# A recurrent mixer in finer steps, its groups four steps apart, with affines and norm scalings on ScalarE and its bias products among the expert tiles of the stage before

## The chip, the cores and the metric

One core of a Trainium2 chip. The time is the device time of one execution in microseconds, the median over several executions of the same program. Stretches of the program are given in microseconds from the first instruction of the profiled execution.

## The reference, cut to what matters

The whole is a decoder of two layers on x of 16 x 128 x 256 (2048 tokens of 256 features), everything in float32. The parts that the change touches are the end of the first layer and the recurrent mixer that opens the second:

```python
out = jnp.einsum('bse,bsem->bsm', gate, y)          # 2 of 16 experts; y holds the bias b2 of each
x = _layernorm(x + out)

xn = _ln(x, ln1_g, ln1_b)
xp = _shift(xn)                                     # the token before
k = (xn * mix_k + xp * (1.0 - mix_k)) @ Wk          # likewise v, and r under a sigmoid
wkv = _wkv(k, v, time_decay, time_first)            # a = ew*a + exp(k)*v; b = ew*b + exp(k); a / (b + 1e-8)
x = x + r * wkv @ Wo
yn = _ln(x, ln2_g, ln2_b)
yp = _shift(yn)
kk = jnp.square(jax.nn.relu((0.5 * yn + 0.5 * yp) @ Wfk))
rr = jax.nn.sigmoid(yn @ Wfr)
x = _layernorm(x + (x + rr * (kk @ Wfv)))           # the outer residual and norm, as the kernel orders them
```

The two layer norms in a row, the one after the experts and the mixer's own ln1, read the same x. The weights that choose an expert's output also weigh its bias: that part is gate (2048 x 16) times b2 (16 x 256), the "bias products" below.

## The kernel before, in words

The kernel writes out every engine's instruction stream by hand, with semaphores between the engines, and divides the program into stages with a barrier on all five queues between them (barrier, L154). An engine carries out its stream in order. Two stages matter.

**The expert stage** (tensor_bank L1021, scalar_bank L1056, vector_bank L1076, gpsimd_bank L1097, sync_bank L1107) works through NT0 = 47 tiles of 128 gathered token rows, each with one expert's weights of 2 MB. Step k of TensorE does the second layer of tile k-5 (bank 6 or 7), the first layer of tile k-3 (banks 2 to 5) and the two transposes of tile k-2 (L1053), which go into bank i % 2 with i = k-2. VectorE, in its step k, applies half of the first layer's relu (four instructions of 128x128, L1086) and then copies the transposes out of their bank (L1095). Results go to the DRAM tensor ys0.

**The mixer** (tensor_mix L1160, scalar_mix L1228, gpsimd_mix L1260, vector_mix L1290) treats the 2048 tokens as four groups of 512 (four blocks of 128 tokens; a group is four sequences). Each group goes through the phases 0 to 13 of steps_e (L1151): step n holds phase n - 2g of group g, so a group runs two steps behind its predecessor. The phases:

- 0, 1: POOL gathers the two expert rows of each token from ys0, eight indirect transfers of 128 rows.
- 2: TensorE multiplies gate by b2 (two banks, two products of 16x128 by 16x256 each); VectorE adds them to X (L1305), adds the eight weighted gathered blocks (L1314), and takes the statistics of the norm (norm_stats L163: four BATCH_NORM_STATS2, four aggregates, variance plus epsilon); POOL raises to the power -0.5 (norm_rstd L176, L181).
- 3: VectorE scales X by the norm (norm_scale L183, L188), takes statistics again; POOL the power. 4: VectorE scales into e_xn.
- 5: TensorE transposes e_xn (na); VectorE applies gain and bias (the affine, L1332), subtracts the token before (L1336) and mixes three times (L1343).
- 6: TensorE multiplies by the k, v and r weights; ScalarE takes exponentials (L1239 to L1244); VectorE multiplies, scans twice (L1354, L1355), adds 1e-8 (L1357), multiplies by 1 + e_r (L1361), takes the reciprocal (L1363) and multiplies (L1368): wkv, in two halves m.
- 7: TensorE's output product (wo); VectorE adds it to X (xi, L1378) and takes statistics, POOL the power. 8: VectorE scales into e_xn; POOL adds xi to X (L1279).
- 9: transposes (nb); VectorE's affine (L1398) and the sum with the token before (hh, L1402).
- 10: TensorE's fk (8 banks) and fr (2 banks); ScalarE relu (L1252) and tanh (L1258); POOL squares (L1288).
- 11: TensorE's fv; VectorE's two steps x4 (L1411, L1414). 12: statistics and power. 13: VectorE scales X (x5).

Banks of PSUM are taken by use (L82), which returns how often the bank was used before; a product then waits until it has been freed as often. In the mixer they go round by eight in TensorE's order. All matmuls are issued through mm (L142), so the profile puts them on L143; one float32 product makes two records.

```python
def steps_e():
    for n in range(20):
        for g in range(4):
            if 0 <= n - 2 * g <= 13:
                yield g, n - 2 * g
```

Of the kernel before, what the change touches and what calls it, by code (L numbers as in the profile page):

```python
# [51 lines left out]
ROWS = ["w2_b", "bo", "br", "gb"]  # L52

# [12 lines left out]
def build(nc, ins, out):  # L66
    with ExitStack() as ctx:
# [1078 lines left out]
        e_th = [alloc(512) for _ in range(2)]  # L1146
        yg_in = [sem(f"yg_in{i}") for i in range(8)]
# [3 lines left out]
        def steps_e():  # L1151
            for n in range(20):
                for g in range(4):
                    if 0 <= n - 2 * g <= 13:
                        yield g, n - 2 * g

        def e_tokens(t, kc, dims):
            return view(t, 516 * kc + dims, [[129, 4], [1, 128]])

        def tensor_mix(t):  # L1160
# [6 lines left out]
            for g, ph in steps_e():  # L1167
                if ph == 2:
                    t.wait_ge(late_in, 64)
                    for b2 in range(2):  # L1170
                        b, n = use(("b2", g, b2), at())
                        t.wait_ge(bank_free[b], n)
                        for i in range(2):
                            c = 4 * g + 2 * b2 + i
                            h = mm(t, banks[b][:, i * 256:(i + 1) * 256], GT[0:16, c * 128:(c + 1) * 128], b2r[0:16, :], True, True)
                        h.then_inc(bank_full[b], 1)
                elif ph in (5, 9):
                    what, ready, src = ("na", xa_done, e_xn[0]) if ph == 5 else ("nb", xb_done, e_xn[1])
                    t.wait_ge(ready, g + 1)
                    for kc in range(2):  # L1180
                        b, n = use((what, g, kc), at())
                        t.wait_ge(bank_free[b], n)
                        for i in range(4):
                            h = t.transpose(banks[b][:, i * 128:(i + 1) * 128], src[:, i * 256 + kc * 128:i * 256 + kc * 128 + 128], ident)
                        h.then_inc(bank_full[b], 1)
                elif ph == 6:
# [8 lines left out]
                elif ph == 7:  # L1195
# [8 lines left out]
                elif ph == 10:  # L1204
# [13 lines left out]
                elif ph == 11:  # L1218
# [9 lines left out]
        def scalar_mix(a):  # L1228
# [3 lines left out]
            for g, ph in steps_e():  # L1232
                if ph == 6:
                    for m in range(2):
# [9 lines left out]
                        a.activation(e_r[m], banks[b], ACT.Exp, scale=-1.0).then_inc(bank_free[b], 1)  # L1244
                elif ph == 10:
# [7 lines left out]
                    for b2 in range(2):  # L1253
# [4 lines left out]
                        a.activation(e_th[b2], banks[b], ACT.Tanh, scale=0.5).then_inc(bank_free[b], 1)  # L1258

        def gpsimd_mix(p):  # L1260
            for i in range(2):
                p.memset(e_XN[i], 0.0).then_inc(xn_pads, 1)
            posi = posi0.bitcast(I32)
            for g, ph in steps_e():
                if ph in (0, 1):
                    for i in range(4):
                        slot = 4 * ph + i
# [4 lines left out]
                elif ph in (2, 3, 7, 12):  # L1272
                    norm_rstd(p, 4)
                elif ph == 8:
# [5 lines left out]
                elif ph == 10:  # L1280
# [9 lines left out]
        def vector_mix(v):  # L1290
            held = {}
# [5 lines left out]
            v.wait_ge(xn_pads, 2)  # L1297
            for g, ph in steps_e():
                xg = xrow(g)
                if ph == 2:  # L1300
                    for b2 in range(2):
                        b, n = U["b2", g, b2]
                        v.wait_ge(bank_full[b], n + 1)
                        xx = X[:, g * 1024 + b2 * 512:g * 1024 + b2 * 512 + 512]
                        v.tensor_tensor(xx, banks[b], xx, ALU.add).then_inc(bank_free[b], 1)  # L1305
                    for kk in range(2):
                        for i in range(4):
                            if kk == 0:
                                b, n = U["b2", g, i // 2]
                                v.wait_ge(bank_free[b], n + 1)  # L1310
                            else:
                                v.wait_ge(summed, 8 * g + i + 1)
# [3 lines left out]
                    held[g] = norm_stats(v, 4, xg)  # L1316
                elif ph == 3:
                    norm_scale(v, held[g], 4, xg, xg).then_inc(vstep.up(), 1)
                    v.wait_ge(vstep.sem, vstep.n)
                    held[g] = norm_stats(v, 4, xg)  # L1320
                elif ph == 4:
# [3 lines left out]
                    norm_scale(v, held[g], 4, xg, lambda i: e_xn[0][:, i * 256:(i + 1) * 256]).then_inc(xa_done, 1)  # L1325
                elif ph == 5:
                    xn = e_XN[0]
                    for kc in range(2):
                        b, n = U["na", g, kc]
                        v.wait_ge(bank_full[b], n + 1)  # L1330
                        v.wait_ge(vstep.sem, vstep.n)
                        v.tensor_scalar(e_tokens(xn, kc, 1), view(banks[b], 0, [[128, 4], [1, 128]]), vcol("g1", kc), vcol("b1", kc), ALU.mult, ALU.add).then_inc(bank_free[b], 1)  # L1332
# [13 lines left out]
                elif ph == 6:  # L1346
                    for m in range(2):
# [8 lines left out]
                        v.wait_ge(vstep.sem, vstep.n)  # L1356
                        v.tensor_scalar(e_b[m], e_b[m], 1e-8, None, ALU.add).then_inc(vstep.up(), 1)  # L1357
# [3 lines left out]
                        v.scalar_tensor_tensor(e_b[m], e_r[m], 1.0, e_b[m], ALU.add, ALU.mult).then_inc(vstep.up(), 1)  # L1361
# [8 lines left out]
                elif ph == 7:  # L1370
                    xi = e_xi[g % 2]
                    if g >= 2:
                        v.wait_ge(xi_added, g - 1)
                        v.wait_ge(xb_done, g - 1)
                    for b2 in range(2):
# [6 lines left out]
                    held[g] = norm_stats(v, 4, lambda i: xi[:, i * 256:(i + 1) * 256])  # L1382
                elif ph == 8:
                    xi = e_xi[g % 2]
                    if g >= 1:
                        b, n = U["nb", g - 1, 1]
                        v.wait_ge(bank_full[b], n + 1)
                    norm_scale(v, held[g], 4, lambda i: xi[:, i * 256:(i + 1) * 256], lambda i: e_xn[1][:, i * 256:(i + 1) * 256]).then_inc(xb_done, 1)
                elif ph == 9:
                    xn = e_XN[1]  # L1390
                    if g >= 1:
                        b, n = U["fr", g - 1, 1]
                        v.wait_ge(bank_full[b], n + 1)
                        v.wait_ge(hh_done, g)
                    for kc in range(2):
                        b, n = U["nb", g, kc]
                        v.wait_ge(bank_full[b], n + 1)
                        v.tensor_scalar(e_tokens(xn, kc, 1), view(banks[b], 0, [[128, 4], [1, 128]]), vcol("g2", kc), vcol("b2", kc), ALU.mult, ALU.add).then_inc(bank_free[b], 1)  # L1398
# [5 lines left out]
                elif ph == 11:  # L1404
# [10 lines left out]
                elif ph == 12:  # L1415
                    v.wait_ge(x4_added, 2 * g + 2)
                    held[g] = norm_stats(v, 4, xg)
                elif ph == 13:
                    norm_scale(v, held[g], 4, xg, xg).then_inc(vstep.up(), 1)
# [666 lines left out]
        NORMS = 48  # L2086
        shift = alloc(16)
        shifted, scaled = sem("shifted"), sem("scaled")
# [59 lines left out]
        def scalar_experts(a):  # L2148
# [24 lines left out]
            for c in range(16):  # L2173
                st = stats[(NORMS + c) % 6]
                a.wait_ge(shifted, c + 1)
# [3 lines left out]
                a.wait_ge(scaled, c + 1)  # L2179
                a.dma_start(out[c * 128:(c + 1) * 128, :], xt2_ring[c % 3]).then_inc(o_out[c % 3], 16)  # L2180

        def vector_experts(v):
# [33 lines left out]
            for u, c in steps_i():  # L2216
                xx = xblock(c)
                if u == "sum":
# [7 lines left out]
                    if c >= 6:  # L2226
                        v.wait_ge(scaled, c - 5)
# [241 lines left out]
```

## Time and profile before

| | us |
|---|---|
| median of three runs | 1712.78 |
| lowest, highest | 1711.32, 1714.36 |
| the profiled execution | 1711.79 |
| its span, first to last instruction | 1709.8 |
| PE (TensorE matmul) busy in it | 1438.0 |
| DVE (VectorE) busy | 916.3 |
| ACT (ScalarE) busy | 542.5 |
| POOL (GpSimd) busy | 514.6 |

The mean granted clock of TensorE was 0.919 of full speed. A chain lists, in order of time, the work that led to the last instruction, each piece with what released the next; "issue" is time in which the engine waited for nothing that the profile shows. In a timeline the bracket gives how long the engine had been idle before an instruction and who ended it. In windows PEclk is the clock that was granted.

### The profile page before, as it was taken

Reading aid. Unit: us, or ns where it says so; the run is one execution under the profiler, and the core shown is the slowest. Engines: PE = TensorE matmul, PEld = TensorE weight load, DVE = VectorE, ACT = ScalarE, POOL = GpSimd, SP = SyncE. Lnnn points to the kernel's source line nnn. Section 1 sums busy time; section 2 is a strip of 40 time slices with the busy share of each in tenths; the row PEclk is TensorE's granted clock in tenths of the full one; section 3 lists DMA queues with packets and bytes.
Section 4 is the critical chain, followed back from the end, with each engine's and each line's share of the span. In section 5 each row is a group of like instructions: output and inputs, shape, how many; then the busy total and the mean of one; then the engine's idle time right before and its main releaser. Section 6 shows DMA issues by size and latency. Waiting matters only on the chain.

```text
span 1709.8 us, 29284 instructions
## 1 busy us (share of the span) xinstructions
PE 1438.0 (84%) x10056; PEld 1108.8 (65%) x10056; DVE 916.3 (54%) x2612; ACT 542.5 (32%) x1377; POOL 514.6 (30%) x506
## 2 busy tenths in 40 slices
PE   7778997569999999646999869988888675999987
PEld 3454676459999999523567535655556443899985
DVE  7353556522222111389776236677768752667655
ACT  4203443212222222000221115443434312666652
POOL 2011000021111110243322211133435473766775
PEclk9888999579999999767999979999999887999998
DMA  7771000079988998110000061112222599655528
GB/s 221 198 239 50 2 15 14 25 291 358 327 319 332 325 326 317 37 50 25 0 1 1 0 177 35 44 65 78 90 80 103 197 317 336 185 175 166 168 69 344
DMA packets 135424, 260.88 MB, mean 153 GB/s; under 512 B 13807, under 2 KB 108043, under 8 KB 129008
## 3 DMA queue, kind: packets, MB, share of 16 engines
q1 hardware_dynamic: 113872, 212.85, 37.0%
q0 software_dynamic: 16800, 39.88, 6.8%
q10 hardware_dynamic: 4608, 6.29, 1.1%
q8 instruction: 82, 1.34, 0.3%
q14 instruction: 62, 0.51, 0.1%
HBM read 197.71 MB, written 52.72 MB: 146 GB/s over the span
## 4 chain that ended last, share of the span: by engine, by line
PE 48%; DVE 10%; issue 8%; POOL 6%; DMA 5%; ACT 1%; SPq 1%; POOLq 0%; ACTq 0%; DVEq 0%
PE bank L143 45%; POOL xe L1556 4%; DMA arena<-in_banka 2%; PE bank L2100 2%; DMA arena<-yr 1%; DVE arena L168 1%; DVE arena L188 1%; DVE arena L1363 1%; POOL arena L1271 1%; DVE arena L1854 1%; SPq L2307 1%; PE bank L1053 1%; POOL arena L181 1%; DVE arena L1844 1%; DMA arena<-xd,arena 0%
## 5 line engine op out<-in xcount | busy, mean ns | idle before, releaser
L143 PE MATMUL bank<-arena 128*128 128x128 f32 (+8 forms) x8728 | 1295.0, 339 | 171.3 <-DMA arena<-in_banka 26.0
L143 PEld LDWEIGHTS bank<-arena 128*128 128x128 f32 (+5 forms) x8728 | 966.7, 181 | 452.2 <-issue 283.4
L181 POOL TENSOR_TENSOR arena<-arena 128x1 f32<-128x1 f32 (+1 forms) x64 | 55.3, 865 | 500.5 <-DVE arena L173 500.5
L1086 DVE TENSOR_SCALAR arena<-bank,arena 128x128 f32<-128x128 f32 x188 | 52.9, 344 | 272.1 <-PE bank L143 272.1
L2241 POOL DMA_INDIRECT yr<-arena x159 | 169.0, 1063 | 95.4 <-ACT arena L2171 49.5
L1105 POOL DMA_INDIRECT arena<-xd,arena x47 | 44.7, 950 | 294.7 <-PE bank L1053 260.9
L1556 POOL DMA_INDIRECT xe<-arena x112 | 113.1, 1010 | 31.6 <-issue 31.5
L2206 DVE COPY arena<-arena 128x768 f32 x127 | 77.0, 607 | 57.2 <-issue 56.9
L1756 ACT ACTIVATE arena<-bank,arena 128x256 f32<-128x256 f32 x128 | 59.0, 472 | 97.7 <-DVE arena L1844 97.7
L1073 ACT ACTIVATE arena<-bank,arena 128x128 f32<-128x128 f32 x188 | 53.7, 368 | 89.8 <-PE bank L143 89.8
L1064 ACT ACTIVATE arena<-bank 128x256 f32<-128x256 f32 x47 | 18.1, 384 | 201.4 <-PE bank L143 201.4
L2171 ACT ACTIVATE arena<-bank,arena 128x256 f32<-128x256 f32 x159 | 73.8, 474 | 23.7 <-PE bank L143 17.7
L2164 ACT ACTIVATE arena<-bank 128x128 f32<-128x128 f32 x143 | 39.7, 278 | 104.9 <-PE bank L143 104.8
L2100 PE MATMUL bank<-arena 128*128 128x128 f32 x318 | 61.1, 282 | 4.3 <-DMA arena<-xe 4.3
L168 DVE BATCH_NORM_STATS2 arena<-arena 128x6 f32<-128x256 f32 x160 | 58.5, 415 | 2.4
L746 DVE TENSOR_REDUCE arena<-bank 128x4 f32<-128x512 f32 x64 | 39.7, 684 | 36.4 <-PE bank L143 36.4
L188 DVE TENSOR_SCALAR arena<-arena 128x256 f32<-128x256 f32 x144 | 53.9, 430 | 10.0 <-POOL arena L181 9.6
L1252 ACT ACTIVATE arena<-bank 128x512 f32<-128x512 f32 x32 | 19.1, 597 | 125.4 <-PE bank L143 97.1
L1796 POOL TENSOR_TENSOR arena<-arena 128x512 f32<-128x512 f32 x16 | 20.3, 1266 | 118.1 <-DVE arena L1835 118.1
L1829 DVE COPY arena<-bank 128x512 f32<-128x512 f32 x16 | 11.1, 692 | 80.2 <-PE bank L143 80.2
L2157 ACT ACTIVATE arena<-bank 128x256 f32<-128x256 f32 x127 | 48.8, 384 | 0.6 <-issue 0.4
L2190 DVE TENSOR_SCALAR arena<-arena 128x1 int32<-128x1 f32 x159 | 32.3, 204 | 27.4 <-DMA arena<-xe 27.3
(243 smaller groups left out, 1371.6 us busy)
## 6 DMA issues: line engine op xcount, KB each, us to landing
arena<-in_bank SPq DMA_DIRECT2D x47, 2052.0 KB
arena<-xe SPq DMA_DIRECT2D x159, 129.0 KB, 2.2
arena<-kd SPq DMA_DIRECT2D x16, 1024.0 KB, 10.9
arena<-arena SPq DMA_DIRECT2D x16, 896.0 KB, 5.4
arena<-in_bank SPq DMA_DIRECT2D x8, 1536.0 KB, 12.0
arena<-yr SPq DMA_DIRECT2D x16, 768.0 KB, 15.0
xe<-arena SPq DMA_DIRECT2D x1, 6321.0 KB, 26.7
ys<-arena SPq DMA_DIRECT2D x47, 128.0 KB, 3.2
```

The lines of the kernel that those rows point to most:

```text
L143: return t.matmul(o, l, r, start=start, stop=stop, skip_group_check=True)
L168: h = v.bn_stats(st[:, 6 * b:6 * b + 6], src(b)).then_inc(vstep.up(), 1)
L181: p.tensor_tensor(st[:, 40:40 + nb], st[:, 32:32 + nb], cc("mhalf", 0, nb), ALU.pow).then_inc(rstd, 1)
L188: h = v.tensor_scalar(dst(b), src(b), st[:, 24 + 2 * b:25 + 2 * b], st[:, 40 + b:41 + b], ALU.subtract, ALU.mult)
L1073: h = a.activation(h_ring[i % 3][:, m * 128:(m + 1) * 128], banks[b][:, m * 128:(m + 1) * 128], ACT.Relu, bias=sbc(w_ring[i % 5], 4096 + m))
L1086: h = v.tensor_scalar(h_ring[i % 3][:, (4 + m) * 128:(5 + m) * 128], banks[b][:, m * 128:(m + 1) * 128], sbc(w_ring[i % 5], 4100 + m), 0.0 ...
L1556: p.indirect_dma_start(xe, bass.IndirectOffsetOnAxis(ap=posi[i][:, at:at + 1], axis=0), stg[i][:, at * RW:(at + 1) * RW], None).then_inc(a ...
L1756: h = a.activation(f_s[g % 2][:, hh * 512 + j * 256:hh * 512 + j * 256 + 256], banks[b][:, j * 256:j * 256 + 256], ACT.Exp, scale=-1.0, bi ...
L2100: h = t.transpose(banks[b][:, (2 * i + j) * 128:(2 * i + j) * 128 + 128], x2_ring[n % NX][:, j * 128:(j + 1) * 128], ident)
L2171: a.activation(y2_ring[n % NY], banks[b][:, 0:256], ACT.Copy, scale=wcol_[:, n:n + 1]).then_inc(bank_free[b], 1)
L2206: v.tensor_copy(e_ring[m % 4], WB[:, bass.ds(at * ROW1, ROW1)]).then_inc(w_copied, 1)
L2241: p.indirect_dma_start(yr, bass.IndirectOffsetOnAxis(ap=sidx.bitcast(I32)[:, n:n + 1], axis=0), y2_ring[n % NY], None, bounds_check=14335, ...
```

## The change

What it does, part by part:

1. **The order.** steps_e goes; a written list MIXER takes its place, of units "0load", "0sum", ... (group, unit). Every engine walks the same list and carries out its part of each unit. A group now stands some four steps behind its predecessor, and a phase is divided into several units.
2. **Biases.** The bias products leave the mixer and are spread over the expert stage, a pair of them at k = 4, 8, ..., 32 behind the transposes, with VectorE's addition behind its copy.
3. **Norms.** The two norms at the start take their statistics once: POOL's power works on eight columns, four for the norm and four for both norms together, with the variance v(1 + eps) + eps^2. Statistics get a buffer for each group and norm.
4. **ScalarE.** The three scalings x3, xb and x5 (four instructions of 128x256) and the two affines (two of 128x512) go to ScalarE, and the 1 + of the sigmoid too. VectorE makes a 128x4 shift for each scaling. The scaling into e_xn ahead of na (xa) stays on VectorE.
5. **wkv.** The 1e-8 is added in the multiplication (one instruction less in each half).
6. **The pads** of e_XN are cleared by VectorE, only where they are read, and no longer by POOL.

```diff
+MIXER = """
+0load 0sum 0xa 0na 0aff 1load 0x3 1sum 0mix 1xa 0kvr 1na 0exp 1aff
+2load 0wkv 1x3 2sum 0wo 1mix 2xa 0xi 1kvr 2na 0xx 1exp 2aff 3load
+0xb 1wkv 2x3 3sum 0nb 1wo 2mix 3xa 0afb 1xi 2kvr 3na 0hh 1xx
+2exp 3aff 0fk 1xb 2wkv 3x3 0sq 1nb 2wo 3mix 0fv 1afb 2xi 3kvr
+0x4 1hh 2xx 3exp 0x5 1fk 2xb 3wkv 1sq 2nb 3wo 1fv 2afb 3xi
+1x4 2hh 3xx 1x5 2fk 3xb 2sq 3nb 2fv 3afb 2x4 3hh 2x5 3fk
+3sq 3fv 3x4 3x5"""
...
(tensor_bank, at the end of step k)
+                for p2 in biases_at(k):
+                    t.wait_ge(late_in, 64)
+                    b, n = use(("b2", p2), k % 2)
+                    t.wait_ge(bank_free[b], n)
+                    for i in range(2):
+                        c = 2 * p2 + i
+                        h = mm(t, banks[b][:, i * 256:(i + 1) * 256], GT[0:16, c * 128:(c + 1) * 128], b2r[0:16, :], True, True)
+                    h.then_inc(bank_full[b], 1)
+        def biases_at(k):
+            return (k // 4 - 1,) if k % 4 == 0 and 0 <= k // 4 - 1 < 8 else ()
...
(vector_bank, at the end of step k)
+                for p2 in biases_at(k):
+                    v.wait_ge(xd0_out, 64)
+                    b, n = U["b2", p2]
+                    v.wait_ge(bank_full[b], n + 1)
+                    xx = X[:, p2 * 512:p2 * 512 + 512]
+                    v.tensor_tensor(xx, banks[b], xx, ALU.add).then_inc(bank_free[b], 1)
...
(scalar_mix)
+            def scaled_by(g, c, src, dst):
+                st = st_of(g, c)
+                a.wait_ge(shifted, shifts[g, c] + 1)
+                for i in range(4):
+                    h = a.activation(dst(i), src(i), ACT.Identity, scale=st[:, 40 + i:41 + i], bias=st[:, 48 + i:49 + i])
+                return h
...
+                        a.activation(e_tokens(e_XN[0], kc, 1), view(banks[b], 0, [[128, 4], [1, 128]]), ACT.Identity, scale=vcol("g1", kc), bias=vcol("b1", kc)).then_inc(bank_free[b], 1)
...
-                        a.activation(e_r[m], banks[b], ACT.Exp, scale=-1.0).then_inc(bank_free[b], 1)
+                        a.activation(e_r[m], banks[b], ACT.Exp, scale=-1.0).then_inc(astep.up(), 1)
+                        a.wait_ge(astep.sem, astep.n)
+                        a.activation(e_r[m], e_r[m], ACT.Identity, bias=cc("ones", 0, 1)).then_inc(bank_free[b], 1)
...
(vector_mix)
-                        v.tensor_scalar(e_b[m], e_b[m], 1e-8, None, ALU.add).then_inc(vstep.up(), 1)
...
-                        v.scalar_tensor_tensor(e_b[m], e_r[m], 1.0, e_b[m], ALU.add, ALU.mult).then_inc(vstep.up(), 1)
+                        v.scalar_tensor_tensor(e_b[m], e_b[m], 1e-8, e_r[m], ALU.add, ALU.mult).then_inc(vstep.up(), 1)
...
+            def shift_of(g, c):
+                st = st_of(g, c)
+                v.scalar_tensor_tensor(st[:, 48:52], view(st, 24, [[2, 4]]), -1.0, st[:, 40:44], ALU.mult, ALU.mult).then_inc(shifted, 1)
```

In the list, "fk" is the fr product too, "sum" holds the gathered sums with their statistics and power, "xi" and "x4" hold theirs, "xx" is POOL's addition of xi to X. TensorE's own order comes out as 0na 0kvr 1na 0wo 1kvr 2na 0nb 1wo 2kvr 3na 0fk 1nb 2wo 0fv 3kvr 1fk 2nb 3wo 1fv 2fk 3nb 2fv 3fk 3fv. The last stage's norm counter starts at 44 instead of 48, and its semaphores shifted and scaled, which the mixer now uses too, at 12 and 4.

## Rows read from the trace of the kernel before

**Rows 1.** Expert stage, ten-microsecond window: busy PE, PEld, DVE, ACT, POOL; clock, DMA, GB/s.

```profile
560.00:570.00 10.00, 10.00 (x70) 9.41 (x69) 2.91 (x10) 2.04 (x7) 1.89 (x2) 1.00 0.94 321
```

**Rows 2.** Chain that ended last, in the expert stage: start us, us, what.

```profile
561.06 0.22 PE bank L1053 x2
561.28 7.03 PE bank L143 x48
```

**Rows 3.** Chain that ended last, in the mixer.

```profile
707.95 1.86 POOL arena L1262 x2
...
818.41 43.21 PE bank L143 x136
...
866.82 41.30 PE bank L143 x136
...
912.48 31.28 PE bank L143 x112
```

**Rows 4.** Timeline, 940 to 990 us: start, us, instruction, idle before.

```profile
943.86 0.69 DVE L1411 SCALAR_TENSOR_TENSOR arena<-arena,bank 128x512 f32<-128x512 f32 x1 [5.46 <-PE bank L143]
...
946.63 1.28 DVE L1402 TENSOR_TENSOR arena<-arena 128x512 f32<-128x512 f32 x2
947.83 1.40 DVE L168 BATCH_NORM_STATS2 arena<-arena 128x6 f32<-128x256 f32 x4
947.96 0.46 PEld L143 LDWEIGHTS bank<-arena 128*128 128x128 f32 x2 [3.58 <-DVE arena L1402]
947.96 32.96 PE L143 MATMUL bank<-arena 128*128 128x512 f32 x112 [3.34 <-DVE arena L1402]
...
949.67 0.17 DVE L173 TENSOR_SCALAR arena<-arena 128x4 f32<-128x4 f32 x1
...
951.91 0.19 PEld L143 LDWEIGHTS bank<-arena 128*128 128x128 f32 x1 [0.24 <-issue]
...
985.63 1.38 DVE L188 TENSOR_SCALAR arena<-arena 128x256 f32<-128x256 f32 x4 [1.12 <-POOL arena L181]
...
988.32 0.23 DVE L1804 CAST arena<-arena 128x128 f16<-128x128 f32 x1 [1.31 <-POOLq L156]
```

**Rows 5.** Half-microsecond windows of L1095, VectorE's copy, alone.

```profile
562.00:562.50 0.50, 0.28 (x1) 1.00 0.92 394
562.50:563.00 0.50, 0.13 (x1) 1.00 1.12 460
```

**Rows 6.** Timeline of all engines from 700 to 760 us.

```profile
729.69 0.95 POOL L1271 DMA_INDIRECT arena<-ys,arena  x1 [0.30 <-issue]
...
735.87 0.95 POOL L1271 DMA_INDIRECT arena<-ys,arena  x1 [0.30 <-DVE arena L1314]
...
741.42 1.53 DVE L1332 TENSOR_SCALAR arena<-bank,arena 128x512 f32<-128x512 f32 x2
...
744.19 4.06 DVE L1343 SCALAR_TENSOR_TENSOR arena<-arena 128x512 f32<-128x512 f32 x6
...
751.65 0.69 DVE L1352 TENSOR_TENSOR arena<-bank,arena 128x512 f32<-128x512 f32 x1
...
754.75 0.45 DVE L1357 TENSOR_SCALAR arena<-arena 128x512 f32<-128x512 f32 x1
```

**Rows 7.** Chain of the stretch from 753 to 835 us.

```profile
760.03 0.69 DVE arena L1352
```

**Rows 8.** Timeline of all engines from 784 to 832 us.

```profile
810.42 3.25 DVE L1314 SCALAR_TENSOR_TENSOR arena<-arena 128x256 f32<-128x256 f32 x8
```

**Rows 9.** Two-microsecond windows: PE busy, PEclk, DMA share, GB/s.

```profile
948.00:950.00 2.00, 2.00 (x3) 0.51 0.00 0
950.00:952.00 2.00, 2.00 (x4) 0.64 0.00 0
```

**Rows 10.** Costliest groups on the page: count, busy us, mean ns, idle before.

```profile
L1756 ACT ACTIVATE arena<-bank,arena 128x256 f32<-128x256 f32 x128 | 59.0, 472 | 97.7 <-DVE arena L1844 97.7
```

**Rows 11.** Groups of instructions from 960 to 1010 us, same columns.

```profile
L1739 ACT ACTIVATE arena<-bank,arena 128x512 f32<-128x512 f32 x4 | 3.1, 778 | 30.1 <-PE bank L1575 30.0
```

More of the change, by code:

```diff
@@ L1146, in build @@
         e_th = [alloc(512) for _ in range(2)]
+        e_st = [alloc(64) for _ in range(12)]
         yg_in = [sem(f"yg_in{i}") for i in range(8)]
@@ L1165, in at, with turned @@
                 return turn[0] % 8
[L1167 to L1186, printed above, removed]
+            def turned(what, g, src):
+                for kc in range(2):
+                    b, n = use((what, g, kc), at())
+                    t.wait_ge(bank_free[b], n)
+                    for i in range(4):
+                        h = t.transpose(banks[b][:, i * 128:(i + 1) * 128], src[:, i * 256 + kc * 128:i * 256 + kc * 128 + 128], ident)
+                    h.then_inc(bank_full[b], 1)
+            for g, u in MIX:
+                if u == "na":
+                    t.wait_ge(xa_done, g + 1)
+                    turned("na", g, e_xn[0])
+                elif u == "nb":
+                    t.wait_ge(xb_done, g + 1)
+                    turned("nb", g, e_xn[1])
+                elif u == "kvr":
                     t.wait_ge(w_in[2], 16)
@@ L1258, in scalar_mix, with pow_of @@
                         a.activation(e_th[b2], banks[b], ACT.Tanh, scale=0.5).then_inc(bank_free[b], 1)
+                elif u == "x5":
+                    scaled_by(g, "c", xg, xg).then_inc(astep.up(), 1)
         def gpsimd_mix(p):
-            for i in range(2):
-                p.memset(e_XN[i], 0.0).then_inc(xn_pads, 1)
             posi = posi0.bitcast(I32)
[L1264 to L1267, printed above, removed]
+            def pow_of(g, c, n):
+                st = st_of(g, c)
+                norms["p"] += 1
+                p.wait_ge(variance, norms["p"])
+                p.tensor_tensor(st[:, 40:40 + n], st[:, 32:32 + n], cc("mhalf", 0, n), ALU.pow).then_inc(rstd, 1)
+            for g, u in MIX:
+                if u == "load":
+                    for slot in range(8):
                         if g >= 1:
@@ L1296, in vector_mix, with stats_of @@
                 v.tensor_scalar(view(dec, 512 * m + 1, [[128, 4], [1, 127]]), view(cc("ones"), 0, [[0, 4], [1, 127]]), sbc(sm2, 2 + m), None, ALU.mult).then_inc(vstep.up(), 1)
[L1297 to L1305 removed]
+            held = {}
+            def stats_of(g, c, src):
+                st = st_of(g, c)
+                for i in range(4):
+                    v.bn_stats(st[:, 6 * i:6 * i + 6], src(i)).then_inc(vstep.up(), 1)
+                v.wait_ge(vstep.sem, vstep.n)
+                for i in range(4):
+                    v.bn_aggr(st[:, 24 + 2 * i:26 + 2 * i], st[:, 6 * i:6 * i + 6]).then_inc(vstep.up(), 1)
+                v.wait_ge(vstep.sem, vstep.n)
+                if c == "a":
+                    v.tensor_scalar(st[:, 36:40], view(st, 25, [[2, 4]]), 1.0 + EPS, EPS * EPS, ALU.mult, ALU.add).then_inc(vstep.up(), 1)
+                    v.wait_ge(vstep.sem, vstep.n)
+                v.tensor_scalar(st[:, 32:36], view(st, 25, [[2, 4]]), EPS, None, ALU.add).then_inc(variance, 1)
+                held[g, c] = norms["v"]
+                norms["v"] += 1
+            def shift_of(g, c):
+                st = st_of(g, c)
+                v.scalar_tensor_tensor(st[:, 48:52], view(st, 24, [[2, 4]]), -1.0, st[:, 40:44], ALU.mult, ALU.mult).then_inc(shifted, 1)
+            for g, u in MIX:
+                xg = xrow(g)
+                if u == "sum":
                     for kk in range(2):
                         for i in range(4):
[L1308 to L1311, printed above, removed]
+                            if kk == 1:
                                 v.wait_ge(summed, 8 * g + i + 1)
@@ L1324, in vector_mix @@
                         v.wait_ge(bank_full[b], n + 1)
-                    norm_scale(v, held[g], 4, xg, lambda i: e_xn[0][:, i * 256:(i + 1) * 256]).then_inc(xa_done, 1)
-                elif ph == 5:
-                    xn = e_XN[0]
[L1328 to L1332, printed above, removed]
+                    v.wait_ge(rstd, held[g, "a"] + 1)
+                    for i in range(4):
+                        h = v.tensor_scalar(e_xn[0][:, i * 256:(i + 1) * 256], xg(i), st[:, 24 + 2 * i:25 + 2 * i], st[:, 44 + i:45 + i], ALU.subtract, ALU.mult)
+                    h.then_inc(xa_done, 1)
+                    shift_of(g, "a")
+                elif u == "mix":
+                    xn = e_XN[0]
                     for kc in range(2):
```

118 lines of the change are left out of this document (70 added, 48 removed).

## The prediction

> **What bounds the kernel now.** The page's forty slices show TensorE at nine tenths from 360 us on and a dip between about 700 and 820 us. I therefore read two stretches: the expert stage that the biases move into, and the mixer that they leave.
>
> In the ten-microsecond windows of the expert stage TensorE is busy all the time at full clock, VectorE for 3 of 10 us and the DMA engines at 0.94 [rows 1]. The chain of waits confirms it: 7.03 us of matmuls, then two transposes of 0.22 us, again and again [rows 2]. TensorE ends the stage, with no slack: what its queue has to sit out there, the kernel pays.
>
> The mixer runs from the barrier at 707.95 to that at 988.32 us [rows 3, 4], 280.4 us. Its chain has two halves. Up to 818.41 us it goes through VectorE, for 110.5 us. From there TensorE runs through: a piece of 43.21 us, one of 41.30, one of 31.28, transposes and output products between them [rows 3]. Then it waits once for VectorE, until 947.96 us [rows 4].
>
> **The biases' move.** Eight times a pair of bias products goes from the mixer's ph 2 into tensor_bank, behind the transposes of tile k-2 for k = 4, 8, ..., 32. Each takes bank k % 2, which for even k is the very bank those transposes have just filled. So TensorE has to wait until VectorE has emptied it. Today nobody is behind that copy: TensorE goes on with the second layer of an earlier tile. The transposes end at 561.28 us [rows 2] and the copy (L1095) at 562.63: it fills the last 0.28 us before 562.5 and 0.13 us after [rows 5]. TensorE would stand for 1.35 us. Behind the waiting product in its queue is everything: second layer, first layer, next transposes.
>
> The products themselves are four records of 256 columns. The piece of 41.30 us holds 56 records of 512 columns and 80 of 256, as much as 192 of 256, so 0.215 each [rows 3], and four are 0.86 us. The restart adds one weight load, 0.19 us at full clock [rows 4]. One insertion is 1.35 + 0.19 + 0.86 = 2.4 us, eight are **+19.2 us**. Bounds: 8 x 0.86 = 6.9 if the stand costs nothing; 8 x 2.65 = 21 if the wake-up takes a quarter more. I take 19.2, since the two rows are of this very place. VectorE's add of 0.68 us in the stage goes into its idle seven tenths. The clock should hold: the rate is at 0.51 from 948 us on only, after a stand of 4.2 us [rows 4, 9]. Nor does anything behind a waiting product slip past it: in that stand TensorE has no record.
>
> The restart after that stand [rows 4] shows the weight load beginning at 947.96 us, together with the matmul and only when the releaser is done. The Trainium skill (TensorE: Matmul & The Clock Gate, section "Step-by-step: what each phase is for") says that the queue pulls weight loads ahead of matmuls in flight, while matmuls stay in order. By that rule the load would hide in the wait and eight insertions would cost 1.5 us less. The row decides for the sum.
>
> In the mixer the same eight pairs cost TensorE nothing today, since they lie in its idle stretches before 818 us; what leaves there is VectorE's eight adds.
>
> **The mixer, first half.** A chain through POOL and VectorE.
> - POOL's two memsets (1.86 us) and 0.15 behind them go, VectorE's small ones stand in idle time: the first gather starts 2.0 us earlier [rows 3].
> - Group 1's eight gathers now follow one power without another in between. The eighth began at 735.87 us; the first four stay at their spacing (the fourth at 729.69), and four more at 1.25 us bring it to 734.7, less 2.0 = 732.7: 3.2 us earlier [rows 6]. The first group's mix waits behind group 1's sum in VectorE's queue, so it gains these 3.2.
> - The affine ahead of the mix (1.53 us [rows 6]) goes to ScalarE: the mix starts 4.65 us earlier.
> - In each half of wkv the addition (0.45 us and a gap of 0.1 [rows 6]) goes: a half took 760.03 - 751.65 = 8.38 us and falls to 7.8 [rows 6, 7]. Group 0's wkv ended at 760.03 + 8.4 = 768.4, 60.5 us into the mixer, and now ends 5.7 earlier, at 54.8.
> - Then VectorE has, up to group 1's wkv: sum 3.25, statistics 2.05 and 0.2 for the wider variance, mix 5.3 (742.95 to 748.25 us), scale 1.6, xi 1.3 (like hh, two of 128x512) and its statistics 2.05, a power of 1.1 waited for, the shift 0.2 [rows 4, 6, 8]; with gaps of 0.7 that is 17.8. The shift (128x4) is in no row; L173, also 128x4, takes 0.17, and between nothing and 0.5 it moves the chain by under 1 us.
> - Group 1's wkv 15.6; group 3's sum and statistics 5.5; the subtraction and first mix of group 2, 2.7. At 96.4 us TensorE gets group 2's k/v/r products, 12 of 0.86 = 10.3, and group 3's transposes 0.9, and begins group 0's fk at 107.6; I take 108. Before, 110.5: **-2.5 us**.
>
> **The mixer, second half.** Group 2's k/v/r products are by now done; before, they came after 818 us: **-10.3**. The first piece before took 43.21, the same work one group on 41.30: the clock had to come back first. Now TensorE comes from 10 us of work at full clock: **-1.9**.
>
> Behind group 1's fv, though, the new order puts group 2's fk at once, and that needs hh, which VectorE does after group 1's x4. VectorE's list is x4 1.4, statistics 2.05, hh 1.28, with the handoffs 4.8 us [rows 4]. The old order had the next group's transposes, output products and k/v/r there. The same happens once more at group 3. Before there was one such stand, from 943.8 to 947.96, 4.2 us, and 4 us at 0.51 and 0.64 of the clock behind it (half rate is 1.2 GHz, full 2.4), 1.7 us lost [rows 4, 9]. One of 5.9 becomes two of 6.5: **+7.1**.
>
> **The tail.** Before, after the last matmul: x4, statistics, power, four scales of 1.38 together, barrier 1.3 [rows 4]. Now a shift of 0.2 and a hand-over, and the scales on ScalarE. L1756, of the same form but from a bank, has 0.472 [rows 10]; overlapping, four make 1.7. **+0.6**. The Trainium skill (ScalarE: Activation LUTs, "What ACT_TABLE_LOAD costs") gives by its formula 0.59 us for 256 elements with two pointer operands, 2.1 for four overlapping: 0.4 more than the row makes, too little to move the forecast. Its rules for authors also want additions and products on VectorE; here an affine of 128x512 takes VectorE 0.8 (half of 1.53) and ScalarE 0.778 [rows 6, 11], so by the trace the moved work is no dearer, and by the rule it would be.
>
> ScalarE gets some 9.5 us a group: 1.6 + 1.6 for affines, 3 x 1.7 for scales, 1.2 to 1.6 for the sigmoid's one. It had seven to nine tenths idle. Before group 0's squares it now has about 6 us of other work once 3na is through; the products are ready after 1.7. POOL then squares in 8 x 1.1 us and is done some 15.5 us after fk began; fv is due after 17.1 + 4.3. The cover is 6 us; without it each fv comes late.
>
> Mixer: -2.5 - 10.3 - 1.9 + 7.1 + 0.6 = **-7.0**, from 280.4 to 273.4 us. Bounds: -12 if the clock holds through both stands and the chain comes a microsecond or two shorter; -2 if chain and handoffs are 5 us worse. Nothing else moves: the last stage merely counts its semaphores from 12 and 4.
>
> **Sum.** 19.2 - 7.0 = +12.2. The profiled execution took 1711.79 us (span 1709.8), so 1724.0 for one like it; against the median of the runs, 1712.78, 1725.0.
>
> **The rivals.**
> - **The insertion is free of the wait** (bank 0 is emptied in time, or TensorE runs something else): then 6.9 - 7.0, 1712.7 us, no change. Against it: the two rows of the transposes' end and the copy's. For it: only that the end of a matmul is modelled. 0.08.
> - **Faster.** VectorE stays ahead of TensorE from group 1's k/v/r on, at 63 us into the mixer. A group's work on TensorE without biases is 28 products of 0.86, 48 of 0.43 and 16 transposes of 0.11, 46.5 us; of the four groups' 186 some 15.5 are done by then. 63 + 170.5 + 13 + 8 = 254.5, 25.9 less than before, and 1706.1 us in all. It decides where VectorE needs less between two wkv than TensorE has to do. Against it: from there to group 2's mix VectorE still has over 33 us against 16 of TensorE's. 0.04.
> - **ScalarE becomes late.** Its queue is in order, with a group's scales ahead of the next one's squares. If the cover of 6 us is gone at each fv, some 2 us a group, the mixer gains nothing: 1732 us. For it: six new kinds of entries in one queue. Against it: the durations above. 0.11.
>
> **How the numbers follow.** The forecast has 0.77. Its own range is 17 to 21 for the insertions and -12 to -2 for the mixer, 1718 to 1732. The range given, 1717 to 1733, takes in the late ScalarE and leaves out the free insertion and the faster case. Within 0.2% (3.4 us, about what a measurement can tell from no change) lies most of the free insertion, 0.06; faster by more, 0.04 + 0.01; slower 0.89.
>
> **What would show it.** In the expert stage of the new profile eight rounds of 9.6 us instead of 7.25, with TensorE idle 1.3 to 1.5 us behind L1095's releaser. Group 0's fk near 108 us into the mixer; no idle TensorE until after group 1's fv; two stands of about 5 us that VectorE's hh ends; the mixer 273 us long. If the eight rounds take 8.1 us the step on the wait is wrong; if TensorE waits for ScalarE or POOL ahead of an fv, the one on the cover; if there is no stand at groups 2 and 3, the one on the order.

## The result and the profile after

The changed kernel took 1740.95 us, the median of 4 runs (1737.12 to 1743.04), against 1712.62 before (1711.32 to 1714.36): a ratio of 1.0159, 95% interval 1.0139 to 1.0178. It is slower, as forecast, but by 28.3 us where 12.2 were forecast, outside the range. The profiled execution took 1739.29 us, with a span of 1737.5.

On the page of the changed kernel, the share of each engine:

```profile
span 1737.5 us, 29256 instructions
PE 1447.2 (83%) x10056; PEld 1114.3 (64%) x10056; DVE 887.6 (51%) x2522; ACT 582.9 (34%) x1449; POOL 519.7 (30%) x500
```

The shares hide the answer; the stages give it. The chain of waits of the changed kernel (start us, us, what), in the mixer:

```profile
736.38 0.18 issue
736.56 0.94 POOL arena L1343
...
826.73 6.13 PE bank L153 x16
832.86 2.19 issue
835.05 12.23 PE bank L153 x24
847.28 0.87 PE bank L1204 x8
848.15 17.19 PE bank L153 x48
...
866.22 44.76 PE bank L153 x152
...
911.85 17.28 PE bank L153 x80
...
932.60 1.31 DVE arena L1480 x2
933.91 0.04 issue
933.95 19.15 PE bank L153 x48
...
971.28 1.30 DVE arena L1480 x2
972.58 0.04 issue
972.63 6.58 PE bank L153 x8
...
1014.15 0.23 DVE arena L1882
```

The mixer's barrier falls at 736.38 us instead of 707.95 [rows 3], **+28.4**, all of it in the expert stage. The mixer ends at 1014.15 and has 277.8 us instead of 280.4: **-2.6**, forecast -7.0. What follows it has 723.3 us instead of 721.5. The profiles of the experiments below have 718.9 to 723.0 there (but four of them, on a slower chip, 778.5 to 788.3), so that is scatter.

The +28.4 sits in the rounds, from one tile's transposes to the next's. Before, and in this kernel without an insertion, a round takes 7.25 us; the eight with one take 10.0 (four) or 11.72 (four), 2.78 and 4.47 more. Four of each make 29.0. Timeline of the changed kernel, an insertion at tile 20:

```profile
500.65 0.38 PE L1063 MATMUL bank<-arena 128*128 128x128 f32 x2
500.93 1.13 DVE L1108 TENSOR_SCALAR arena<-bank,arena 128x128 f32<-128x128 f32 x4 [5.79 <-PE bank L153]
501.97 0.41 DVE L1117 COPY arena<-bank 128x256 f32<-128x256 f32 x1
502.50 0.72 PEld L153 LDWEIGHTS bank<-arena 16*128 16x128 f32 x4 [1.70 <-issue]
502.53 10.01 PE L153 MATMUL bank<-arena 16*128 16x256 f32 x52 [1.50 <-DVE arena L1117]
...
512.37 0.38 PE L1063 MATMUL bank<-arena 128*128 128x128 f32 x2
...
519.61 0.38 PE L1063 MATMUL bank<-arena 128*128 128x128 f32 x2
```

Transposes, then VectorE's copy out of the bank (L1117), and nothing on TensorE until 502.5. The stand (time in which TensorE waits with all its later work behind it) is there, 1.50 us. The record after it holds the four bias products and the 48 matmuls that take 7.19 us in a round without an insertion. It takes 10.01. The granted clock is in the one-microsecond windows of TensorE (window: length, busy, PEclk, DMA share, GB/s) at the same place:

```profile
501.00:502.00 1.00, 0.03 (x1) 1.00 0.83 345
502.00:503.00 1.00, 0.47 (x2) 1.00 0.92 378
503.00:504.00 1.00, 1.00 (x5) 0.98 0.97 410
504.00:505.00 1.00, 1.00 (x4) 0.50 1.04 427
505.00:506.00 1.00, 1.00 (x4) 0.50 0.67 271
506.00:507.00 1.00, 1.00 (x4) 0.50 0.20 82
507.00:508.00 1.00, 1.00 (x5) 0.81 0.02 8
```

After the stand and the products the clock is at 0.50 (1.2 GHz) for some 3.4 us. Half the work of 3.4 us is 1.7 us, by which 11.72 exceeds 10.03. The forecast put that term at nothing.

### The profile page after: what moved, and what is told of

It reads as the page before. It is cut to its first block, busy times and chain, and to the rows that moved or that the text cites. A ratio compares the mean times of both kernels' runs of the same rounds, so it can differ in the third digit from the quotient of the medians.

```text
span 1737.5 us, 29256 instructions
## 1 busy us (share of the span) xinstructions
PE 1447.2 (83%) x10056; PEld 1114.3 (64%) x10056; DVE 887.6 (51%) x2522; ACT 582.9 (34%) x1449; POOL 519.7 (30%) x500
## 4 chain that ended last, share of the span: by engine, by line
PE 28%; issue 9%; DVE 8%; POOL 6%; DMA 4%; SPq 2%; ACT 1%; POOLq 0%; ACTq 0%; DVEq 0%
PE bank L153 25%; POOL xe L1634 4%; PE bank L2178 2%; DMA arena<-in_banka 2%; DMA arena<-yr 1%; DVE arena L1448 1%; DVE arena L1932 1%; DVE arena L198 1%; SPq L2385 1%; SPq L2356 1%; DVE arena L1922 1%; SPq L2357 1%; DVE arena L178 0%; POOL arena L191 0%; POOL arena L1874 0%
## 5 line engine op out<-in xcount | busy, mean ns | idle before, releaser
L191 POOL TENSOR_TENSOR arena<-arena 128x1 f32<-128x1 f32 (+1 forms) x48 | 37.2, 776 | 333.2 <-DVE arena L183 333.2
L1095 ACT ACTIVATE arena<-bank,arena 128x128 f32<-128x128 f32 x188 | 53.7, 368 | 90.4 <-PE bank L153 90.4
L1335 POOL TENSOR_TENSOR arena<-arena 128x4 f32<-128x4 f32 (+1 forms) x12 | 17.4, 1449 | 134.8 <-DVE arena L1388 134.8
L1874 POOL TENSOR_TENSOR arena<-arena 128x512 f32<-128x512 f32 x16 | 20.2, 1265 | 118.7 <-DVE arena L1913 118.7
L1343 POOL DMA_INDIRECT arena<-ys,arena x32 | 32.4, 1011 | 60.5 <-SPq L166 51.5
L1364 POOL TENSOR_TENSOR arena<-arena 128x512 f32<-128x512 f32 x32 | 37.9, 1203 | 34.1 <-ACT arena L1318 34.1
L2288 DVE TENSOR_TENSOR arena<-bank,arena 128x128 f32<-128x128 f32 x143 | 41.1, 288 | 12.3 <-ACT arena L2242 8.8
```

The source lines that it names most:

```text
L1095: h = a.activation(h_ring[i % 3][:, m * 128:(m + 1) * 128], banks[b][:, m * 128:(m + 1) * 128], ACT.Relu, bias=sbc(w_ring[i % 5], 4096 + m))
L2288: v.tensor_tensor(h2_ring[m % 3], banks[b][:, 128:256], h2_ring[m % 3], ALU.mult).then_inc(bank_free[b], 1)
```

## The experiments

The theory after the result: each insertion costs 1.66 us of stand and 1.25 of products, and at about half of them stand and products make TensorE's clock fall. The rivals: something else that the change put into the stage slows it; the products alone cost the clock; the mixer's new order costs too. Times are medians, ratios against the kernel before on the same chip. What is said of rounds and of the mixer is read from one profiled execution of each kernel.

**The bank.** The products take the bank that the transposes have not just filled.

```
-                    b, n = use(("b2", p2), k % 2)
+                    b, n = use(("b2", p2), (k + 1) % 2)
```

> The changed kernel with the eight bias insertions in bank (k + 1) % 2 = 1, emptied long ago, instead of the bank that VectorE is just emptying. Theory (the wait for the bank): TensorE's stand of 1.5 us before each pair goes, the products of about 1.1 us stay, so eight rounds of 8.3 us instead of 10.0 or 11.7 and the expert stage 20 us shorter: 1721 us in all. Rival 1 (the clock is lost because of the products, which fill 16 of 128 rows, and not because of the stand): four of the eight rounds stay at about 10 us, 7 us more, 1728 us. Rival 2 (the rounds are longer because the weight loads come late): nothing changes, 1741 us.

1722.89 us (1721.2 to 1725.17), ratio 1.0068 (1.0053 to 1.0083). All eight rounds take 8.50. Timeline of this kernel:

```profile
402.81 0.38 PE L1063 MATMUL bank<-arena 128*128 128x128 f32 x2
...
403.12 0.72 PEld L153 LDWEIGHTS bank<-arena 16*128 16x128 f32 x4 [0.17 <-issue]
403.13 8.35 PE L153 MATMUL bank<-arena 16*128 16x256 f32 x52
...
404.13 0.42 DVE L1117 COPY arena<-bank 128x256 f32<-128x256 f32 x1
...
411.31 0.38 PE L1063 MATMUL bank<-arena 128*128 128x128 f32 x2
```

The products run while the copy (L1117) is still to come. No stand, no loss of clock, 18 us back of 28 with one character. What is left is 8 x 1.25, the products.

**The biases back in the mixer**, with all else of the change kept.

```
-            return (k // 4 - 1,) if k % 4 == 0 and 0 <= k // 4 - 1 < 8 else ()
+            return ()
...
+                if u == "sum":
+                    t.wait_ge(late_in, 64)
+                    for b2 in range(2):
...
```

> The changed kernel with the bias products and additions back in the mixer, in the unit sum; the expert stage is then that of before. Theory: the expert stage falls back by 28.4 us and all its rounds are 7.25 us; in the mixer VectorE has 1.3 us more for each of groups 0 to 3, some 4 us on the path, so the mixer is 280 to 283 us and the whole 1715 to 1718 us. Rival (half or more of the loss lies in the mixer or behind it): 1725 us or more.

1713.9 us (1710.56 to 1715.56, 12 runs), ratio 1.0007 (0.9997 to 1.0017). All rounds are 7.25 again. The mixer has 281.6 us, 3.8 more than the changed kernel's: that is all that taking the biases out of it was worth. So the new order, with the affines and scalings on ScalarE, gains nothing by itself that a run can tell.

**The stand alone**: the kernel above, with TensorE waiting for the copy where the products stood, and no products.

```
+                if k % 4 == 0 and 0 <= k // 4 - 1 < 8:
+                    b, n = U["tr0", k - 2]
+                    t.wait_ge(bank_free[b], n + 1)
```

> Like the run with the biases back in the mixer, but TensorE still waits at the eight places until VectorE has emptied the bank of the transposes, with no product behind the wait. Theory: 1.5 to 1.7 us a place, 13 us over that run. If it is the stand that costs the clock, four of the eight places cost 1.7 us more and it is 20 us over it; if it is the products of 16 rows (rival), every one of the eight rounds is 8.8 to 8.9 us.

1729.45 us (1725.93 to 1731.18), ratio 1.0098 (1.0078 to 1.0118); eight rounds of 8.91 (one of them 8.84), +1.66 each, and none longer. The windows behind the stand at 406 us:

```profile
406.00:407.00 1.00, 0.02 (x1) 1.00 0.82 328
407.00:408.00 1.00, 0.57 (x3) 1.00 0.97 394
```

The clock holds over the bare stand, so a stand of this length alone is not what lowers it. The whole is 15.6 us over the run with the biases back, where 13 were expected: the eight rounds make 13.3, and the first of them began 1.9 us later.

**Stand and products, with all 128 rows.** The products run over 16 rows of weights and biases. Here they run over all 128, the other rows of the biases being zero: the same count of columns, the same stand.

```
+            p.memset(b2r, 0.0).then_inc(pads, 1)
...
-                        h = mm(t, banks[b][:, i * 256:(i + 1) * 256], GT[0:16, c * 128:(c + 1) * 128], b2r[0:16, :], True, True)
+                        h = mm(t, banks[b][:, i * 256:(i + 1) * 256], GT[:, c * 128:(c + 1) * 128], b2r, True, True)
```

> The changed kernel with the bias products over all 128 rows (b2r cleared beyond its 16, the rows of GT as they lie) instead of 16: as many columns, as long a stand, the same bank. Theory (the clock falls where a stand of 1.5 us and products on 16 rows come together; neither alone did it): no round of 11.7 us is left, eight of 10.0 us, and the whole is 7 us shorter, 1734 us. Rival (it is the total time in which the rows are idle or waiting, whatever the products fill): four or five rounds of 11.7 us again, 1741 us.

1796.29 us (1791.58 to 1801.36), ratio 1.0135 (1.0094 to 1.0177), on a chip on which all four kernels profiled there had slower stages behind the mixer (1771.26 us for the kernel before). The rounds decide: all eight take 9.77 to 9.84 us, none 11.72. The windows at one of them:

```profile
404.00:405.00 1.00, 0.00 (x0) 1.00 0.95 394
405.00:406.00 1.00, 0.95 (x5) 1.00 1.03 443
406.00:407.00 1.00, 1.00 (x6) 1.00 0.99 427
407.00:408.00 1.00, 1.00 (x7) 1.00 0.91 390
```

The same stand, the same number of products, and the clock stays at 1.00. With the runs before, this is a table: the stand alone, no fall; 16-row products alone, none; the stand and 128-row products, none; the stand and 16-row products, a fall at 4 of 8. At this length of stand it took both. That holds for this place only: in the mixer of the changed kernel the clock also falls behind a stand of 2.19 us ahead of 128-row products (0.50 from 835.06 us on). The number of falls varies (4 in the changed kernel's profile, 5, 6, 5 and 6 in those of the four experiments that keep the insertion as it is). Two falls more or less would make 3.4 of the 6 us by which the changed kernel's runs differ. Stand and products are as long at the places that fall as at those that don't (10.03 us of round without the fall), and all 26 falls of the five profiles begin 2.6 to 4.2 us after the round's first transpose. So it looks like a matter of when an insertion comes; no run moved it by a known amount, and why some of the eight fall stays open.

**The insertion alone, in the kernel before**: the old mixer and its old order, only its ph 2 pairs moved as the change does.

> The kernel before, with nothing changed but the biases' place: products and additions among the expert tiles as in the changed kernel, the mixer otherwise in its old order. Theory (the loss is made in the expert stage, whatever the mixer does): rounds of 10.0 and 11.7 us at the eight places, the expert stage 28 us longer, the mixer 4 to 6 us shorter for the eight additions that leave VectorE: 22 to 24 us over the kernel before. Rival (the loss needs the new mixer, as by a barrier that is reached later by another queue): under 10 us over it.

1740.68 us (1738.32 to 1745.2), ratio 1.0159 (1.0133 to 1.0184), the changed kernel's ratio. Six of the eight rounds take 11.6 to 11.72, two 10.03. Its timelines at the two barriers:

```profile
739.01 1.85 POOL L1270 MEMSET arena<- 128x1032 f32 x2 [51.26 <-SPq L156]
...
1017.04 0.23 DVE L1804 CAST arena<-arena 128x128 f16<-128x128 f32 x1 [1.31 <-POOLq L156]
```

The mixer has 278.0 us, 2.4 less than before; 4 to 6 less had been expected, and the whole is 27.8 us over the kernel before where 22 to 24 had been: besides the mixer there are six falls, not four. The insertion is the whole loss, and the rest of the change nets about nothing.

**The shift.** In the mixer one small instruction had grown. Timeline of the changed kernel:

```profile
804.00 0.15 DVE L1394 SCALAR_TENSOR_TENSOR arena<-arena 128x4 f32<-128x4 f32 x1
...
808.54 2.35 POOL L1355 TENSOR_TENSOR arena<-arena 128x1024 f32<-128x1024 f32 x1
808.60 2.30 DVE L1394 SCALAR_TENSOR_TENSOR arena<-arena 128x4 f32<-128x4 f32 x1 [1.12 <-POOL arena L1335]
```

The same instruction, for another group, takes 0.15 us alone and 2.30 beside POOL's addition. It ends when the addition does. The first try puts POOL's addition behind the shift.

```
+                    p.wait_ge(shifted, shifts[g, "b"] + 1)
```

> The changed kernel; POOL's addition of xi to X (128x1024) waits until VectorE's 128x4 shift of the same group is done. Theory (the two block one another: the shift took 2.3 us beside that addition and 0.15 elsewhere): the shifts of groups 0 and 1 take 0.15 us, group 1's and 2's wkv start 2.1 us earlier each, group 0's fk starts 4 us earlier, and the whole is 4 us shorter, 1737 us. Rival (the addition then blocks the first instruction of wkv as long, or the shift was late for another reason): within 1 us of 1741.

1738.6 us (1737.34 to 1744.18), ratio 1.0169 (1.0147 to 1.019), and 278.1 us of mixer instead of 277.8: no gain. Its timeline:

```profile
811.97 0.16 DVE L1395 SCALAR_TENSOR_TENSOR arena<-arena 128x4 f32<-128x4 f32 x1 [1.12 <-POOL arena L1335]
...
812.30 2.35 POOL L1356 TENSOR_TENSOR arena<-arena 128x1024 f32<-128x1024 f32 x1 [0.37 <-DVE arena L1395]
...
812.77 2.96 DVE L1442 TENSOR_TENSOR_SCAN arena<-arena 128x512 f32<-128x512 f32 x1
```

The shift is short again and the scan behind it long, 2.96 us instead of 1.22. The block had only moved.

**The addition beside the reciprocal.** POOL's addition stands later in the list and waits until VectorE starts its 3.35 us reciprocal, which reads one operand.

```
+                    if g < 3:
+                        p.wait_ge(conv_done, 8 + 2 * (g + 1) + 1)
...
+                        v.engine_nop().then_inc(conv_done, 1)
```

> The changed kernel; POOL's addition of xi to X stands later in the list and waits until VectorE begins the reciprocal of the next group's first wkv half. Theory (POOL's 128x1024 addition blocks those VectorE instructions that read two operands from SBUF, shift and scan, and not the reciprocal, which reads one; moving it by a shift alone only moved the block to the scan): shift 0.15 us, scan 1.2 us, reciprocal 3.35 us, group 2's k/v/r and group 0's fk start 3 to 4 us earlier, the whole 3 to 4 us shorter, 1737 us. Rival (it blocks the reciprocal too): reciprocals of 5.5 us beside it and nothing gained.

1804.43 us (1801.51 to 1805.5), ratio 1.0183 (1.015 to 1.0216), on the chip of 1771.26. Timeline of group 0's addition, which came late behind POOL's gathers, then of group 1's:

```profile
819.65 2.47 POOL L1357 TENSOR_TENSOR arena<-arena 128x1024 f32<-128x1024 f32 x1
820.09 2.58 DVE L1448 SCALAR_TENSOR_TENSOR arena<-arena 128x512 f32<-128x512 f32 x1
...
848.00 3.35 DVE L1451 RECIPROCAL arena<-arena 128x512 f32<-128x512 f32 x1
...
848.18 2.36 POOL L1357 TENSOR_TENSOR arena<-arena 128x1024 f32<-128x1024 f32 x1 [4.20 <-DVEq L1450]
```

At 848 both run at once and neither is longer than alone. At 820 the addition came too late for the reciprocal that it was meant for (812.93) and met a multiply of two operands, 2.58 us instead of 0.69. Group 1's first reciprocal came 2.1 us earlier (76.2 us into the mixer instead of 78.3) and the second no longer did (86.0 to 86.2). The mixer has 277.7 us: no gain. The mechanism held, the placing failed.

**hh ahead of x4.** The two stands of 4.8 us in the changed kernel (929.13 to 933.95 and 967.80 to 972.63 us in its chain, the successors of the one in [rows 4]) wait for VectorE's x4, statistics and hh, but hh needs nothing of the other group's x4.

```
-1x4 2hh 3xx 1x5 2fk 3xb 2sq 3nb 2fv 3afb 2x4 3hh 2x5 3fk
+2hh 1x4 3xx 1x5 2fk 3xb 2sq 3nb 2fv 3afb 3hh 2x4 2x5 3fk
```

> The changed kernel with group 2's hh ahead of group 1's x4 in the list, and group 3's ahead of group 2's x4. Theory: the two stands of 4.8 us in TensorE (fk waits for a hh that VectorE does behind x4 and its statistics) go, and with them 1.7 us of lost clock each; TensorE runs through from group 0's fk to the last fv. 13 us less than the changed kernel, 1728 us. Rival (ScalarE, which now meets the scaling x5 of the group before ahead of the squares, is then late by as much): less than 4 us gained, 1737 us or more.

1790.22 us (1785.22 to 1796.15) against 1771.26, ratio 1.011 (1.0079 to 1.0142); the mixer has 265.3 us, 12.5 less than in the changed kernel (the kernel just above has 277.7 on this very chip). Its timeline, around what was the first stand:

```profile
915.19 34.62 PE L153 MATMUL bank<-arena 128*128 128x256 f32 x128
...
921.58 1.29 DVE L1480 TENSOR_TENSOR arena<-arena 128x512 f32<-128x512 f32 x2
...
932.73 0.69 DVE L1489 SCALAR_TENSOR_TENSOR arena<-arena,bank 128x512 f32<-128x512 f32 x1 [5.46 <-PE bank L153]
```

hh (L1480) is done before the x4 (L1489) that used to stand ahead of it, and TensorE runs through here. The two stands (9.7 us) and the clock lost behind them are gone: 1.7 us behind the first and 2.9 behind the second, where the changed kernel is at 0.50 until 978.4. One new stand of 1.71 us has come, at 950.68: ahead of an fv TensorE waits for POOL's squares, which wait for ScalarE, which does a scaling first. That is the late ScalarE of the expectation, at 1.7 us. 9.7 + 4.6 - 1.7 is 12.6, the 12.5 measured. The clock stays at 1.00 behind that stand. The whole is 19.0 us over the kernel before, where 15 had been expected; this profile has six falls in the expert stage, two more than the changed kernel's.

**Three together**: the biases back, hh first, the addition beside the reciprocal.

> Biases back in the mixer (the run of 1713.9 us), hh ahead of x4 and POOL's addition beside the reciprocal. Theory: the three parts add up: 1713.9 - 13 - 3.5 = 1697 us, 15 us faster than the kernel before. Rival (with the stands gone ScalarE or the squares bound the second half): 1705 us or more.

1761.26 us (1754.32 to 1770.45, 12 runs) against 1771.26, ratio 0.9941 (0.992 to 0.9963). The mixer has 266.4 us. Expected was a gain of 15, it was 10. Group 0's addition missed its reciprocal again (2.58 us for the multiply beside it), and the new stand of 1.7 us is here too. In the last kernel that addition waits for the second reciprocal.

```
-                        p.wait_ge(conv_done, 8 + 2 * (g + 1) + 1)
+                        p.wait_ge(conv_done, 8 + 2 * (g + 1) + (2 if g == 0 else 1))
```

> As the combined version (biases in the mixer, hh ahead of x4, POOL's addition beside a reciprocal), with group 0's addition waiting for the second half of group 1's wkv instead of the first: there POOL's gathers had held it back until it ran into a VectorE instruction of two operands (2.58 us instead of 0.69). Theory: that instruction is back at 0.7 us, the mixer is 2 us shorter, 264 us, and the whole stands 16 us under the kernel before, a ratio of 0.990 to 0.992. Rival (gathers or other POOL work block VectorE as much): the mixer stays at 266 us.

1700.36 us (1694.29 to 1707.12, 6 runs) against 1712.92, ratio **0.9927** (0.9905 to 0.9949): it beats both kernels. The mixer has 265.7 us, where 264 were expected, 14.7 less than before, and the whole gains 12.6 us, where 16 were. The multiply is back at 0.69 us, but against the kernel above the mixer gives only 0.7 us: the placing of group 0's addition is worth little. By the runs above the biases' place and hh's are what matters (1713.9 less 12.5 would be 1701.4); a kernel with these two alone was not run.

## Why the prediction was wrong, and where it was right

The direction, the place and the wait were right; a stage that TensorE fills paid for every microsecond that its queue stood. The size was wrong, by 16.1 us: 9.2 of them are the expert stage (28.4 for 19.2) and 4.4 the mixer (-2.6 for -7.0); the other 2.5 are the last stages (+1.8) and the medians against the profiled runs.

**The step that failed is "The biases' move", at "The clock should hold".** It took one fall of the trace, after a stand of 4.2 us, as the point from which falls begin, and priced a stand of 1.35 at nothing. Measured are stands of 1.50 us with the clock at 0.50 behind four of eight, and four falls at 1.69 make 6.8 us. The trace of the kernel before had falls behind much shorter stands than 4.2 us, outside the two stretches that were read. One is at 118.6 us, behind 1.97 us; TensorE's timeline and its windows there:

```profile
118.45 4.73 PE L143 MATMUL bank<-arena 128*128 128x256 f32 x13 [1.97 <-DVE arena L468]
```

```profile
119.00:120.00 1.00, 1.00 (x4) 0.50 0.00 0
```

The step bounded the wake-up, but not the clock, and the upper end of 21 rested on that. A stand that no row shows needed the loss of rows 4 and 9, 1.7 us, as its other bound: 8 x 1.7 more than 19.2 would have put the insertions' upper end at 32.8, which takes in the 28.4.

- The products were put at 0.86 by columns. Without a stand they measured 1.25, with one 1.12 (2.78 less 1.66), and over 128 rows some 0.93 (2.59 less 1.66); what the difference to 0.86 consists of was not tried. The forecast took it from columns of 128-row products. The stand was put at 1.35 + 0.19 and measured 1.66. Together 8 x 0.38 = 3.0 us; with the 6.8 of the clock that is 9.8, of which the stage's earlier start took back 0.6. In the changed kernel the weight load begins at 502.50, behind the copy, together with the matmul: the rule of the Trainium skill (TensorE: Matmul & The Clock Gate, "Step-by-step: what each phase is for") by which a load is pulled ahead of matmuls in flight does not reach over a semaphore wait here, as the row before had it.
- **First half of the mixer**: group 0's fk begins 111.8 us in (848.15 less 736.38); before it was 110.5, and the working gave 107.6. +1.3 instead of -2.5. The 4.2 us, along the chain: 0.6 up to the end of group 0's wkv, where POOL's power with its eight columns took 1.68 us instead of 1.1; 1.3 between the two wkv, where the shift, priced at 0.2 within 0 to 0.5 because its work is tiny, took 2.30 held up by another engine, and 0.8 of that came back elsewhere; 0.3 in group 1's wkv and 0.2 behind it; and 1.9 at group 2's products, which met a stand of 2.19 us and a lowered clock behind it: 13.1 us from their start at 835.05 to fk instead of 11.2.
- **Second half**: 166.0 us from fk to the barrier against 169.9, **-3.9** where the terms gave -4.5. The two stands are there, 4.82 and 4.83 us for 4.8, both ended by hh (L1480). The clock behind them cost 1.7 us and 2.9, where 1.7 was priced for each. From fk to the end of 1fv are 80.98 us; the order was read rightly.
- **ScalarE was not late.** In the changed kernel TensorE has no idle time of over half a microsecond ahead of any fv. The cover was thin all the same: with hh first one fv came 1.71 us late. Four scales take 2.06 us (L1265) instead of 1.7; the figure by formula that the forecast quoted from the Trainium skill (ScalarE: Activation LUTs, "What ACT_TABLE_LOAD costs"), an estimate of 2.1 for four, was the better one, but it falls where ScalarE is idle.
- **The rival of the free insertion** fell with the first timeline. Its price was low too: without the wait the other bank gave 1722.89 us, not 1712.7, since the products cost 10.0 instead of 6.9 and the mixer and the last stages gave less.
- **The faster rival** stayed away for the reason given: VectorE was the later one up to group 2's mix.

## What to carry to other kernels

Before work is inserted into a loop that one engine fills, look at whose buffer it takes: the bank just written puts the engine behind another's copy, the other bank does not (18 of 28 us here). Even free of the wait the products cost 10 us where TensorE was full; where they had been, they and VectorE's additions cost 3.8. In a queue written by hand, put the short step that the next stage needs ahead of the longer one that nobody waits for (12.5 us), and before pricing a stand at nothing but its length, look through the whole trace for the shortest stand with a fall behind it; where the new one is shorter still, the fall (1.7 us here) is the upper bound.

## What the hardware showed beyond that

- A stand of 1.5 us could cost the clock: stand and 16-row products, 0.50 at 26 of 40 places in five profiles and 1.7 us each; stand and 128-row products, the stand alone, or the 16-row products alone, 1.00 at all eight each. Behind stands of about 2 us it fell with 128-row products too (1.97 us in the kernel before, 2.19 in the changed one).
- While POOL adds two operands of 128x1024 in SBUF (2.35 us), a VectorE instruction with two SBUF operands didn't proceed in these traces: 2.30 for 0.15 (128x4), 2.96 for 1.22, 2.58 for 0.69. The reciprocal, with one, stays at 3.35. The Trainium skill says as much (Advanced Engine Details and Errata, "GPSIMD Details": Pool and VectorE share a read and a write interface, and an instruction of VectorE with two SBUF inputs conflicts), and this case's trace agrees: 2.30 us for 0.15.
